# A local-attention layer with post-norm and a ternary FFN: scores on the whole array, o moved by DMA, FFN bias on ScalarE

## Chip, cores and metric

The kernel runs on one core of one Trainium2 chip. The metric is the device time of one execution in microseconds; the median of three runs is given for the kernel before.

## What is computed

For x of 16 sequences x 512 tokens x 256 features (all float32):

```python
qkv = (x @ Wqkv + bqkv).reshape(B, S, 3, H, Dh)          # 16 heads of 16
# blocks of 128 tokens; a query sees keys at most 128 positions away
scores = einsum('bhnqd,bhnkd->bhnqk', qb, kwin) * (1/16) # masked outside the band
out = einsum('bhnqk,bhnkd->bhnqd', softmax(scores), vwin)
x = layernorm(x + out @ Wout + bout)
h = relu(x @ quantise(W1).T + b1)                        # W1 (1024, 256), values -1, 0, 1
x = layernorm(x + h @ quantise(W2).T + b2)
```

## The kernel before

A **row** is one sequence of 512 tokens. The loop `steps` goes over rows; in the body of row b the attention of row b, the projections of row b+1 and the rest (output projection, norms, FFN) of row b-1 run side by side. One body has four **quads**, v = 0 to 3: quad v makes the scores of four heads of row b, and the row maxima of the four heads that come two quads later. Each quad has 12 **units** of scores (three for a head: blocks of 384, 384 and 2 x 256 columns) and 12 units of maxima; `weave` puts them at positions between the matmuls of the other steps, which the table `SIDE` lists for each quad. Before, positions come in runs of two units of both kinds.

Precision: matmul operands are split in a rounded part and a rest (`_hi`, `_lo`); ScalarE writes the first, VectorE the second, so nearly every PSUM result passes ScalarE and then VectorE before TensorE can use it.

The steps that matter here, with their engines:
- `scores` (L459) multiplies 50 of 128 partitions, `max_scores` (L475) 48 of them. The two lie in different halves of the partitions, since a quad and the one two quads later use different halves c. VectorE then adds the band to a unit of maxima and takes the row maximum (L812), ScalarE takes the exponential of a unit of scores (L670), GpSimd zeroes what is outside the band (`mask`, L973, L977).
- `pva`, `pvb` (L503): probabilities times v for the quad before, four column groups of 32 side by side. ScalarE copies the result to u (L714).
- `ut` (L513): four transposes of u, then VectorE takes the reciprocal of 16 sums per partition (L848) and multiplies (L852). `ot` (L543): eight transposes of the normalised o per row, then oT_hi on ScalarE, oT_lo on VectorE (L859), then the output projection `op` (L484).
- `ln1`, `x1`, `x1t` (L564): statistics on VectorE, rstd on GpSimd, x1 on both ScalarE and VectorE, eight transposes, x1T_hi and x1T_lo.
- `f1` (L578, L582): per 128 hidden units one matmul that adds the bias from a row of ones, then four of 256 columns; relu to hid_hi on ScalarE (L740), rest on VectorE (L895). `f2` (L595): 32 matmuls of 256 columns. `ln2` on VectorE and GpSimd (L1027).
- PSUM: two score banks, three for maxima, three shared by all other steps in turn. SyncE issues all DMAs in program order.

`dve_order` delays a VectorE piece by so many units of maxima as `LAG` says.

Of the kernel before, what the change touches and what calls it, by code (L numbers as in the profile page):

```python
# [21 lines left out]
F32 = mybir.dt.float32  # L22
F32R = mybir.dt.float32r
# [39 lines left out]
]  # L63

COST = {"qk": (3072, 6), "vp": (3072, 12), "op": (3072, 12), "ut": (1024, 4), "ot": (1024, 4), "x1t": (1024, 4),
        "nmt": (256, 1), "f1": (2560, 10), "f2": (8192, 32), "pva": (2200, 1), "pvb": (2200, 1)}
# [4 lines left out]
N_MAX = 3  # L71
RUN = 2
RUNS_AT = (0.5, 0.92)

LAG = {"ln1": 1, "ln2": 1, "qk": 1, "ot": 1, "x1t": 0, "f1": 0, "op": 1, "ut": 0, "f2": 1}
N_SHARED = 6 - N_MAX

USES_BANK = {"pva", "ut", "qk", "ot", "op", "vp", "x1t", "f1", "f2", "nmt"}
# [20 lines left out]
NEEDS = {"ot": "ut", "op": "ot", "f1": "x1t", "f2": "f1"}  # L99


def weave():

    out = []
    for v in range(QUADS):
        total = sum(COST.get(name_of(s), (0, 0))[0] for s in SIDE[v])
        units = []
        for i in range(UNITS):
            pos = (i // RUN * RUN + RUNS_AT[0]) / UNITS * total * RUNS_AT[1]
            units += [(pos, "scores", i), (pos, "max", i)]  # L110
# [11 lines left out]
WOVEN = weave()  # L122

# [9 lines left out]
def row_of(v, step, at):  # L133
# [9 lines left out]
    if name == "xr":  # L143
        return (0, None) if attn else None
# [17 lines left out]
def dve_order(v):  # L162
# [7 lines left out]
    for step, woven in zip(SIDE[v], WOVEN[v]):  # L170
# [9 lines left out]
        after = late[-1][0] + 1 if late and name_of(late[-1][1]) == name_of(step) in ("ln1", "ln2") else 0  # L180
# [12 lines left out]
def postln_layer(nc, xT, x, wqkv, bqk, bv, wout, bout, w1T, b1, w2T, b2, out):  # L193
    ctx = ExitStack()
    with ctx:
# [11 lines left out]
        B1 = sb("b1_rows", [P, FF], F32R)  # L207
        ONES2 = sb("ones_rows", [P, S // 2], F32R)
# [5 lines left out]
        ONES = sb("ones", [P, P])  # L214
# [5 lines left out]
        SK = sb("k_stack", [P, 8, S], F32R)  # L220
# [24 lines left out]
        ABS = sb("abs_sums", [P, 3])  # L245
        THR = sb("thresholds", [P, 4])
# [5 lines left out]
        PST = [bank("st_a"), bank("st_b")]  # L252
# [22 lines left out]
        s_small = sem("bqk_bv_in")  # L275
        s_const = sem("constants")
# [4 lines left out]
        s_b1 = sem("b1_lo_in")  # L281
# [800 lines left out]
```

## Time and profile before

| | |
|---|---|
| median of three runs | 1185.28 us (1185.11 to 1187.25) |
| profiled execution, its own time | 1187.86 us |
| its span | 1186.1 us |
| TensorE matmul busy | 1056.2 us, 89% |
| VectorE busy | 859.3 us, 72% |
| ScalarE busy | 613.3 us, 52% |
| GpSimd busy | 518.8 us, 44% |
| mean granted TensorE clock | 0.924 of full |

Busy time counts compute instructions alone. The clock has two levels, 1.2 GHz (0.5) and 2.4 GHz (1.0); a mean between them says how much of the time each was granted. A matmul's duration in the trace is its latency; how fast matmuls follow each other is read from their starts.

### The profile page before, as it was taken

The page shows a single profiled execution, that of the slowest core. Times are in us where ns is not written, and L with a number is a line of the kernel's source. Part 1 is how long each engine was busy: PE and PEld are TensorE (multiplying, and loading weights), DVE is VectorE, ACT ScalarE, POOL GpSimd, SP SyncE. Part 2 cuts the span into 40 slices and gives each one's busy share as a digit, 9 for nine tenths or more (in the row PEclk, how much of TensorE's full clock was granted, in tenths as well). Part 3 has the DMA queues.
Part 4 walks back from the last instruction along what each step waited for, and adds up shares of the span by engine and source line. Part 5 has one row for each costly group of instructions (what it writes and reads, how often), then busy time and mean ns, then how long its engine had stood idle before and what let it go on. Part 6 is the DMA issues. An engine that isn't in the chain of part 4 may idle for free.

```text
span 1186.1 us, 23520 instructions
## 1 busy us (share of the span) xinstructions
PE 1056.2 (89%) x8132; PEld 771.9 (65%) x8132; DVE 859.3 (72%) x2934; ACT 613.3 (52%) x1258; POOL 518.8 (44%) x824
## 2 busy tenths in 40 slices
PE   4778899999989899998989999898989999897966
PEld 3444676766767576676767666676767667675755
DVE  3975777778787777778777777877777787777333
ACT  4154554655455564556455555545655554555421
POOL 2124353544535445463535445453535445344430
PEclk9677899998989999898999989898998989898889
DMA  5835255434354443444344534424554342442000
GB/s 169 108 54 92 28 82 82 68 70 73 58 75 68 83 73 76 61 80 65 56 82 73 88 61 78 75 37 82 82 82 68 69 74 57 57 69 56 1 19 18
DMA packets 56999, 81.49 MB, mean 69 GB/s; under 512 B 7729, under 2 KB 27697, under 8 KB 56882
## 3 DMA queue, kind: packets, MB, share of 16 engines
q1 hardware_dynamic: 56882, 80.00, 40.3%
q8 instruction: 66, 1.08, 0.4%
q14 instruction: 51, 0.42, 0.2%
HBM read 20.19 MB, written 8.39 MB: 24 GB/s over the span
## 4 chain that ended last, share of the span: by engine, by line
PE 77%; DVE 13%; issue 4%; POOL 2%; ACT 2%; DMA 1%; SPq 0%; POOLq 0%; DVEq 0%; ACTq 0%
PE shared L484 18%; PE st_a L459 13%; PE shared L503 12%; PE shared L595 11%; PE shared L582 10%; DVE mx L812 5%; PE st_b L459 5%; PE shared L578 3%; PE shared L564 3%; DVE oT_lo L859 2%; POOL ln_rstd L1007 1%; PE shared L543 1%; PE mx L475 1%; DVE qk_lo L839 1%; DVE rmax L812 1%
## 5 line engine op out<-in xcount | busy, mean ns | idle before, releaser
L812 DVE CUSTOM_DVE_ANT_0 mx<-mx,band 128x384 f32<-128x384 f32 (+1 forms) x1024 | 480.1, 514 | 187.0 <-PE mx L475 182.6
L670 ACT ACTIVATE probs<-st_a 128x384 f32<-128x384 f32 (+1 forms) x384 | 202.0, 526 | 371.3 <-PE st_a L459 367.7
L475 PE MATMUL mx<-k_stack,q_stack 48*128 48x384 f32 (+1 forms) x1024 | 273.0, 369 | 8.0 <-DMA k_stack<-qk_lo 3.9
L973 POOL TENSOR_SCALAR_AFFINE_SELECT probs<-probs 128x512 f32<-128x512 f32 (+1 forms) x256 | 128.8, 527 | 317.5 <-ACT probs L670 316.3
L670 ACT ACTIVATE probs<-st_b 128x384 f32<-128x384 f32 (+1 forms) x384 | 200.8, 523 | 0.0
L459 PE MATMUL st_a<-q_stack,k_stack 50*128 50x384 f32 (+1 forms) x512 | 186.9, 406 | 3.1 <-ACT probs L670 2.4
L475 PEld LDWEIGHTS mx<-k_stack,q_stack 48*128 48x128 f32 x1024 | 165.7, 201 | 13.2 <-DVE rmax L812 8.7
L503 PE MATMUL shared<-probs,v_aug 128*32 128x384 f32 (+1 forms) x2048 | 161.2, 445 | 0.7 <-DVE x L902 0.7
L459 PEld LDWEIGHTS st_a<-q_stack,k_stack 50*128 50x128 f32 x512 | 90.3, 197 | 104.2 <-issue 63.5
L812 DVE DVE_READ_ACCUMULATOR2_ANT rmax<- 128x1 f32 x1024 | 144.5, 141 | 0.0
L459 PE MATMUL st_b<-q_stack,k_stack 50*128 50x384 f32 (+1 forms) x512 | 143.2, 320 | 0.0
L582 PE MATMUL shared<-x1T_hi,w1q 128*128 128x256 f32 x512 | 142.9, 295 | 0.0
L582 PE MATMUL shared<-x1T_lo,w1q 128*128 128x256 f32 x512 | 138.5, 288 | 0.0
L595 PE MATMUL shared<-w2q,hid_hi 128*128 128x256 f32 x512 | 131.9, 293 | 4.1 <-DVE hid_lo L895 4.1
L595 PE MATMUL shared<-w2q,hid_lo 128*128 128x256 f32 x512 | 131.8, 293 | 0.0
L977 POOL TENSOR_SCALAR_AFFINE_SELECT probs<-probs 128x512 f32<-128x512 f32 (+1 forms) x256 | 127.1, 520 | 0.0
L895 DVE SCALAR_TENSOR_TENSOR hid_lo<-shared,hid_hi 128x512 fp32r<-128x512 f32 x128 | 87.9, 687 | 36.0 <-ACT hid_hi L740 34.6
L740 ACT ACTIVATE hid_hi<-shared 128x512 fp32r<-128x512 f32 x128 | 76.8, 600 | 59.4 <-PE shared L582 59.4
L595 PEld LDWEIGHTS shared<-w2q,hid_hi 128*128 128x128 f32 x512 | 97.7, 191 | 14.7 <-issue 10.2
L582 PEld LDWEIGHTS shared<-x1T_hi,w1q 128*128 128x128 f32 x512 | 99.4, 194 | 10.5 <-issue 7.7
L503 PEld LDWEIGHTS shared<-probs,v_aug 128*32 128x32 f32 x2048 | 57.7, 111 | 68.2 <-issue 50.7
L595 PEld LDWEIGHTS shared<-w2q,hid_lo 128*128 128x128 f32 x512 | 97.4, 190 | 6.9 <-issue 2.9
(107 smaller groups left out, 1965.3 us busy)
## 6 DMA issues: line engine op xcount, KB each, us to landing
q_stack<-qk_hi SPq DMA_DIRECT2D x128, 128.0 KB, 4.3
k_stack<-qk_hi SPq DMA_DIRECT2D x128, 128.0 KB, 5.2
x_raw<-in_xT SPq DMA_DIRECT2D x16, 512.0 KB, 5.7
q_stack<-qk_lo SPq DMA_DIRECT2D x64, 128.0 KB, 3.9
k_stack<-qk_lo SPq DMA_DIRECT2D x64, 128.0 KB, 5.5
y<-in_x SPq DMA_DIRECT2D x16, 512.0 KB, 6.1
out<-x SPq DMA_DIRECT2D x32, 256.0 KB, 2.1
probs<-in_w2T SPq DMA_DIRECT2D x1, 1024.0 KB, 10.6
```

What stands on the lines that cost most here:

```text
L459: mm = pe.matmul(PST[i % 2][:, col:col + n], SK[rows, hd, W * m:W * m + W], SQ[rows, hd, q0:q0 + n], start=True, stop=True)
L475: mm = pe.matmul(PMX[i % N_MAX][:, col:col + n], SQ[rows, hd, W * m:W * m + W], SK[rows, hd, k0:k0 + n], start=True, stop=True)
L484: mm = pe.matmul(ps, lhs(a, kc), rhs(z, kc), start=(n == 0), stop=(n == len(terms) - 1))
L503: mm = pe.matmul(G[32 * g:32 * g + 32, q0:q0 + width], VAUG[:, vq, m, g, :], PR[:, vq % 2, g // 2, lo:lo + width], start=(m == 0), stop=(m ...
L582: mm = pe.matmul(ps, W1Q[:, kc, P * f:P * f + P], X1T[a][:, kc, 256 * hf:256 * hf + 256], start=False, stop=(kc == KC - 1 and a == 1))
L595: mm = pe.matmul(G[:, D * t:D * t + D], HID[a][:, f, P * t:P * t + P], W2Q[:, f, :], start=(f == 0 and a == 0), stop=(f == FC - 1 and a == 1))
L670: act.activation(PR[:, v % 2, g // 2, lo:lo + n], PST[i % 2][:, 0:n], ACT.Exp, scale=SCALE) \
L740: act.activation(HID[0][:, 2 * p:2 * p + 2, :].rearrange("p f t -> p (f t)"), G[:, :], ACT.Relu).then_inc(s_hh, 1)
L812: mx = dve.tensor_tensor_reduce(ps, ps, band, 1.0, -3e38, ALU.add, ALU.max, RMAX[:, g, m:m + 1])
L895: dve.scalar_tensor_tensor(pair[1], G[:, :], 0.0, pair[0].bitcast(F32), ALU.max, ALU.subtract).then_inc(s_hl, 1)
L973: pool.affine_select(out=pr_before, in_=pr_before, compare_op=ALU.is_ge, fill=0.0, base=0, pattern=[[0, n], [1, W]], channel_multiplier=-1)
L977: last = pool.affine_select(out=pr_after, in_=pr_after, compare_op=ALU.is_ge, fill=0.0, base=0, pattern=[[0, n], [-1, W]], channel_multipl ...
```

## The change

- `scores` and `max_scores` use all partitions: k gets one stack for each half, zero in the other half (`SK[0]`, `SK[1]`), so 128 rows (scores) or 112 (maxima) are multiplied. The scores of a quad now also wait for the stacks of the other half.
- Three score banks, three for maxima, two shared. Units stand one by one: `SCORES_AT`, `MAXIMA_AT` in place of runs.
- `ut` and `ot` on TensorE are gone. v lies in the even columns of `VAUG` and ones in the odd ones, so u has o in even partitions and the sums in odd ones; two DMAs per quad (`columns`) bring them to `OC` and `SC`. A new step `od` (twice per row) takes the reciprocal of 128 x 512 sums on VectorE and multiplies: on VectorE for half 1, on GpSimd for half 0. oT_hi and oT_lo read `OC`.
- `f1` has no bias matmul: ScalarE makes relu with bias in two halves (to U or H32), then copies it to hid_hi; VectorE subtracts from SBUF. The shared bank is free after the relu.
- The neg_max transpose goes to a bank of the maxima. ln1's rstd is made in two halves.
- `SIDE` and `LAG` are new.

```diff
 SIDE = [
-    [("qk", 0), "nmt", "pva", "pvb", ("vp", 0), "ut", ("vp", 1), ("ot", 0), ("ot", 1), ("qk", 1), ("op", 0),
-     ("op", 1)],
...
+    [("qk", 0), "nmt", ("ot", 0), "pva", "pvb", ("qk", 1), ("od", 1)],
+    [("ot", 1), ("qk", 2), ("op", 0), ("ln1", 0), ("op", 1), ("ln1", 1), "nmt", ("ln1", 2), ("ln1", 3), ("vp", 0),
+     ("x1", 0), ("x1", 1), "pva", "pvb", ("x1", 2), ("x1", 3), ("qk", 3), ("vp", 1), ("x1t", 0), ("xs", 0),
+     ("x1t", 1)],
+    ["nmt", ("f1", 0, 0), ("f1", 0, 1), ("f1", 0, 2), "pva", "pvb", ("f1", 0, 3), ("xs", 1), ("f2", 0),
+     ("ln2", 0)],
+    [("ln2", 1), ("f1", 1, 0), "xr", ("od", 0), ("f1", 1, 1), ("f1", 1, 2), ("f1", 1, 3), ("f2", 1), ("ln2", 2),
+     "nmt", ("ln2", 3), "pva", "pvb"],
 ]
-LAG = {"ln1": 1, "ln2": 1, "qk": 1, "ot": 1, "x1t": 0, "f1": 0, "op": 1, "ut": 0, "f2": 1}
+LAG = {"ln1": 1, "ln2": 0, "qk": 1, "od": 3, "ot": 1, "x1t": 1, "f1": 0, "op": 2, "f2": 0}
...
+            def columns(r, vq):
+                i, q = vq // 2, 4 * r + vq
+                rows = slice(64 * (vq % 2), 64 * (vq % 2) + 64)
+                sp.wait_ge(s_u, q + 1)
...
+                sp.dma_start(OC[rows, i, :], U[0:P:2, :]).then_inc(s_uin, 16)
+                sp.dma_start(SC[rows, :], U[1:P:2, :]).then_inc(s_uin, 16)
...
-                    mm = pe.matmul(PST[i % 2][:, col:col + n], SK[rows, hd, W * m:W * m + W],
-                                   SQ[rows, hd, q0:q0 + n], start=True, stop=True)
+                    mm = pe.matmul(PST[i % N_SCORE][:, col:col + n], SK[c][:, hd, W * m:W * m + W],
+                                   SQ[:, hd, q0:q0 + n], start=True, stop=True)
...
-                        pe.matmul(ps, B1[:, P * f:P * f + P], ONES2[:, :], start=True, stop=False)
...
+                    for k, f in enumerate((2 * p, 2 * p + 1)):
+                        last = act.activation(H[:, 256 * k:256 * k + 256], G[:, 256 * k:256 * k + 256], ACT.Relu,
+                                              bias=B1C[:, f:f + 1])
+                    last.then_inc(s_hr, 1)
+                    act.wait_ge(s_hr, n + 1)
+                    act.activation(HID[0][:, 2 * p:2 * p + 2, :].rearrange("p f t -> p (f t)"), H[:, :],
+                                   ACT.Identity).then_inc(s_hh, 1)
...
+                elif name == "od":
+                    i = step[1]
+                    dve.wait_ge(s_uin, 128 * r + 64 * i + 64)
+                    dve.reciprocal(SC[:, :], SC[:, :]).then_inc(s_rc, 1)
+                    if i == 1:
+                        dve.wait_ge(s_rc, 2 * r + 2)
+                        dve.tensor_tensor(OC[:, i, :], OC[:, i, :], SC[:, :], ALU.mult).then_inc(s_od, 1)
...
-                    dve.scalar_tensor_tensor(pair[1], G[:, :], 0.0, pair[0].bitcast(F32), ALU.max,
-                                             ALU.subtract).then_inc(s_hl, 1)
+                    dve.tensor_tensor(pair[1], (U, H32)[p % 2][:, :], pair[0].bitcast(F32), ALU.subtract) \
+                        .then_inc(s_hld, 1)
...
+                elif step == ("od", 0):
+                    pool.wait_ge(s_rc, 2 * r + 1)
+                    pool.tensor_tensor(OC[:, 0, :], OC[:, 0, :], SC[:, :], ALU.mult).then_inc(s_od, 1)
```

**Place 1: VectorE, from the end of quad 0 into quad 1, where o is finished** (ISA with mx is a unit of row maxima, rmax its read-out). Before:

```order
L848 RECIPROCAL recip<-shared 128x16 [waits o_norm_done,uT_full]
L852 TENSOR_TENSOR o_norm<-shared,recip 128x4x64 [waits recip_done]
L812 ISA mx,rmax<-mx,band 128x384 [waits max_scores_full]
L812 ISA rmax 128x1
L812 ISA mx,rmax<-mx,band 128x384 [waits max_scores_full]
L812 ISA rmax 128x1
L812 ISA mx,rmax<-mx,band 128x256 [waits max_scores_full]
L812 ISA rmax 128x1
L812 ISA mx,rmax<-mx,band 128x256
L812 ISA rmax 128x1
L859 SCALAR_TENSOR_TENSOR oT_lo<-shared,bv_cols,oT_hi 128x512 [waits oT_hi_done] x2
```

Of the change:

```order
L916 SCALAR_TENSOR_TENSOR qk_lo<-shared,bqk,qk_hi 128x512 [waits qk_hi_done]
L922 RECIPROCAL sums_cols<-sums_cols 128x512 [waits u_and_sums_in]
L925 TENSOR_TENSOR o_cols<-o_cols,sums_cols 128x512 [waits recip_done]
L889 ISA mx,rmax<-mx,band 128x384 [waits max_scores_full,neg_max_done]
L889 ISA rmax 128x1
L929 SCALAR_TENSOR_TENSOR oT_x1T_lo<-o_cols,bv_cols,oT_x1T_hi 128x512 [waits oT_hi_done]
```

Before, a reciprocal of 16 elements stands alone and three units of maxima lie between it and the rests of o. Now one of 512 elements and the multiplication follow the rest of qk1, and the second rest of o comes one unit later.

**Place 2: VectorE, at the start of quad 3, among the rests of the hidden layer.** Before:

```order
L852 TENSOR_TENSOR o_norm<-shared,recip 128x4x64 [waits recip_done]
L895 SCALAR_TENSOR_TENSOR hid_lo<-shared,hid_hi 128x512 [waits hidden_hi_done]
L812 ISA mx,rmax<-mx,band 128x384 [waits max_scores_full,neg_max_done]
L812 ISA rmax 128x1
L812 ISA mx,rmax<-mx,band 128x384 [waits max_scores_full]
L812 ISA rmax 128x1
L895 SCALAR_TENSOR_TENSOR hid_lo<-shared,hid_hi 128x512 [waits hidden_hi_done]
```

Of the change:

```order
L966 TENSOR_TENSOR hid_lo<-u,hid_hi 128x512 [waits hidden_hi_done]
L889 ISA mx,rmax<-mx,band 128x384 [waits max_scores_full]
L889 ISA rmax 128x1
L922 RECIPROCAL sums_cols<-sums_cols 128x512 [waits u_and_sums_in]
L889 ISA mx,rmax<-mx,band 128x256 [waits max_scores_full]
L889 ISA rmax 128x1
L889 ISA mx,rmax<-mx,band 128x256
L889 ISA rmax 128x1
L966 TENSOR_TENSOR hid_lo<-hidden,hid_hi 128x512 [waits hidden_hi_done]
L889 ISA mx,rmax<-mx,band 128x384 [waits max_scores_full]
L889 ISA rmax 128x1
L966 TENSOR_TENSOR hid_lo<-u,hid_hi 128x512 [waits hidden_hi_done]
```

The other reciprocal of 512 elements now stands between the first rest and the other three of this half.

**Place 3: TensorE, from the transposes of x1 to the FFN** (quad 1 into quad 2). Before:

```order
L564 MATMUL shared<-identity,x 128x128
L484 MATMUL shared<-xT_hi,wqkv_hi 128x512 [waits o_norm_done]
L484 MATMUL shared<-xT_hi,wqkv_lo 128x512
L484 MATMUL shared<-xT_lo,wqkv_hi 128x512
L484 MATMUL shared<-xT_hi,wqkv_hi 128x512
L459 MATMUL st_a<-q_stack,k_stack 128x384 [waits exp_done]
L475 MATMUL mx<-k_stack,q_stack 128x384 [waits max_read]
```

Of the change:

```order
L529 MATMUL st<-q_stack,k_stack_top 128x256 [waits exp_done,v_next_done]
L529 MATMUL st<-q_stack,k_stack_top 128x256
L629 MATMUL shared<-identity,x 128x128 x4
L588 MATMUL mx<-identity,neg_max 72x128 [waits neg_max_done]
L643 MATMUL shared<-oT_x1T_hi,w1q 128x256 [waits x1T_lo_done,x1T_hi_done]
L643 MATMUL shared<-oT_x1T_lo,w1q 128x256
L643 MATMUL shared<-oT_x1T_hi,w1q 128x256 [waits x1T_lo_done,x1T_hi_done]
```

Before, the whole projection qk3 and two runs of units lie between the last transpose and the first FFN matmul (L578 follows two more matmuls later). Now only the small transpose of neg_max does.

## Rows read from the trace of the kernel before

**Rows 1.** chain of waits, starts of one row and the next (start us, us, what)

```profile
454.31 0.50 PE shared L484
...
522.50 0.50 PE shared L484
```

**Rows 2.** busy time by stage, one whole row (us, then each engine's busy us, clock, DMA share)

```profile
454.31:522.50 68.19, 63.43 (x508) 46.57 (x509) 52.53 (x183) 37.69 (x78) 32.42 (x51) 0.95 0.44 72
```

**Rows 3.** waits of TensorE in that row, largest first, and the last of five

```profile
PE shared L564 <- ACT x L727: 1.5, 1, 1.5
PE shared L513 <- ACT u L714: 1.4, 1, 1.4
...
PE shared L484 <- DVE qk_lo L839: 0.2, 1, 0.2
```

**Rows 4.** busy time by stage around the transposes of x1 (granted clock third from the right)

```profile
481.20:482.60 1.40, 0.00 (x0) 0.01 (x1) 1.40 (x7) 1.22 (x3) 1.40 (x4) 0.51 0.00 0
...
485.33:488.05 2.72, 2.72 (x11) 1.88 (x11) 1.90 (x7) 1.25 (x3) 2.16 (x1) 0.50 0.01 3
488.05:491.00 2.95, 2.95 (x25) 2.41 (x21) 2.71 (x10) 2.21 (x4) 1.99 (x5) 1.00 0.34 92
```

**Rows 5.** timeline of TensorE, one run of units between FFN matmuls (start us, us)

```profile
500.37 0.28 PE L595 MATMUL shared<-w2q,hid_lo 128*128 128x256 f32 x1
500.49 0.28 PE L595 MATMUL shared<-w2q,hid_hi 128*128 128x256 f32 x1
500.70 0.38 PE L459 MATMUL st_a<-q_stack,k_stack 50*128 50x256 f32 x1
500.71 0.38 PE L475 MATMUL mx<-k_stack,q_stack 48*128 48x256 f32 x1
...
501.04 0.33 PE L459 MATMUL st_b<-q_stack,k_stack 50*128 50x384 f32 x1
...
501.32 0.39 PE L595 MATMUL shared<-w2q,hid_lo 128*128 128x256 f32 x1
501.54 0.28 PE L595 MATMUL shared<-w2q,hid_hi 128*128 128x256 f32 x1
```

**Rows 6.** timeline of TensorE, 512 columns and probabilities times v

```profile
524.29 0.39 PE L484 MATMUL shared<-xT_hi,wqkv_lo 128*128 128x512 f32 x1
524.52 0.39 PE L484 MATMUL shared<-xT_lo,wqkv_hi 128*128 128x512 f32 x1
...
524.95 1.28 PE L503 MATMUL shared<-probs,v_aug 128*32 128x256 f32 x16
526.17 0.38 PE L459 MATMUL st_a<-q_stack,k_stack 50*128 50x256 f32 x1
```

**Rows 7.** chain of waits, the transposes of u and of o

```profile
530.75 0.44 PE shared L513 x4
...
533.35 0.87 PE shared L543 x8
```

**Rows 8.** groups by line and shape (busy us, mean ns | idle before), VectorE, ScalarE, TensorE

```profile
L812 DVE DVE_READ_ACCUMULATOR2_ANT rmax<- 128x1 f32 x1024 | 144.5, 141 | 0.0
...
L895 DVE SCALAR_TENSOR_TENSOR hid_lo<-shared,hid_hi 128x512 fp32r<-128x512 f32 x128 | 87.9, 687 | 36.0 <-ACT hid_hi L740 34.6
...
L578 PE MATMUL shared<-ones_rows,b_rows 128*128 128x256 f32 x256 | 80.8, 315 | 3.8 <-DVE x1T_lo L889 2.0 <-DVE hid_lo L895 0.4
L740 ACT ACTIVATE hid_hi<-shared 128x512 fp32r<-128x512 f32 x128 | 76.8, 600 | 59.4 <-PE shared L582 59.4
...
L852 DVE TENSOR_TENSOR o_norm<-shared,recip 128x256 f32<-128x256 f32 x64 | 27.2, 425 | 2.2
...
L848 DVE RECIPROCAL recip<-shared 128x16 f32<-128x16 f32 x64 | 15.9, 249 | 6.4 <-PE shared L513 6.4
```

**Rows 9.** groups by line and shape, GpSimd: mask and second norm

```profile
L973 POOL TENSOR_SCALAR_AFFINE_SELECT probs<-probs 128x512 f32<-128x512 f32 x128 | 82.9, 647 | 317.5 <-ACT probs L670 316.3
...
L1027 POOL TENSOR_SCALAR x<-x,ln_mv,ln_rstd 128x256 f32<-128x256 f32 x60 | 73.1, 1224 | 3.2
```

More of the change, by code:

```diff
@@ L106, in weave @@
         total = sum(COST.get(name_of(s), (0, 0))[0] for s in SIDE[v])
[L107 to L110, printed above, removed]
+        units = [((i + SCORES_AT[0]) / UNITS * total * SCORES_AT[1], "scores", i) for i in range(UNITS)]
+        units += [((i + MAXIMA_AT[0]) / UNITS * total * MAXIMA_AT[1], "max", i) for i in range(UNITS)]
+        units.sort()
         at, slot = 0, []
@@ L122, with units_before, ffn_steps_in_u @@
 WOVEN = weave()
+def units_before(v, step, kind):
+    return sum(k == kind for woven in WOVEN[v][:SIDE[v].index(step)] for _, k, _ in woven)
+NMT_AT = [units_before(v, "nmt", "max") for v in range(QUADS)]
+assert max(NMT_AT) < UNITS
+def ffn_steps_in_u():
+    out, n, last = [], 0, 0
+    for v in range(QUADS):
+        for step in SIDE[v]:
+            if name_of(step) == "f1":
+                n += 1
+                last = n if step[2] % 2 == 0 else last
+            if step == "pvb":
+                out.append(last)
+    return out
+U_FFN = ffn_steps_in_u()
 def stages(at):
@@ L179, in dve_order @@
                 due(maxima)
-        after = late[-1][0] + 1 if late and name_of(late[-1][1]) == name_of(step) in ("ln1", "ln2") else 0
+        after = late[-1][0] + 1 if late and name_of(late[-1][1]) == name_of(step) == "ln2" else 0
         late.append((max(maxima + LAG.get(name_of(step), 0), after), step))
@@ L449, in scores @@
                 c, hd = v // 2, 4 * (v % 2) + g
-                rows = slice(64 * c, 64 * c + 50)
                 if i == 0:
@@ L466, in max_scores @@
                 c, hd = v // 2, 4 * (v % 2) + g
-                rows = slice(64 * c, 64 * c + 48)
+                rows = slice(0, 112)
                 if i == 0:
@@ L471, in max_scores @@
                     pe.wait_ge(s_mxr, 12 * (4 * r + v) + i - N_MAX + 1)
+                if i == NMT_AT[(v + 2) % 4] and not (first and v == 0):
+                    pe.wait_ge(s_nmt, 4 * r + v)
                 for m in BLOCKS[u]:
@@ L751, in step @@
                             other_weights()
+                        row = row_of(v, step, at)
+                        before = name_of(step) in ("f1", "nmt", "pvb", "x1t")
+                        if row is not None and before:
+                            side_work(v, step, b, *row, at)
                         for _, kind, i in woven:
@@ L754, in step @@
                                 exp(b, v, i, at)
-                        row = row_of(v, step, at)
-                        if row is not None:
+                        if row is not None and not before:
                             side_work(v, step, b, *row, at)
@@ L890, in side_work @@
                         .then_inc(s_x1l, 1)
-                elif name == "f1":
+                elif name == "f1" and step[2] not in REST_ON_POOL:
                     hf, p = step[1], step[2]
```

310 lines of the change are left out of this document (167 added, 143 removed), and 6 rows, old and new, of the table SIDE.

## The prediction

> **What bounds the kernel now.** I read the page first: TensorE is busy 89% of the span, VectorE 72%. The chain of waits gives the period: the same matmul of qk0 starts at 454.31 and at 522.50 us [rows 1], so a row of the batch costs 68.2 us, and 15.5 such rows (the first has no FFN yet, the last no projections) stand between a start and an end of some 50 us each. Within one row TensorE is busy 63.4 us, VectorE 52.5, ScalarE 37.7, at a mean clock of 0.95 [rows 2]. The waits of TensorE inside it are five and sum to 4.7 us; the largest are for x1 and for u [rows 3]. The clock is lost in one place: around the wait for x1 it falls to the 1.2 GHz level, and from 482.6 to 488.05 TensorE works at half rate [rows 4], 5.4 us that would take 2.7. So 68.2 = 60.8 of matmuls at full clock + 4.7 of waits + 2.7 of clock. TensorE bounds the kernel, through its own work and through short chains over ScalarE, VectorE and GpSimd.
>
> **Full-array scores: no gain by themselves.** A score matmul and a maxima matmul start together, at 500.70 and 500.71 us, since they lie in different halves of the array [rows 5]. That is lost. What is won is the passage between half and full array: from the last FFN matmul before the run (500.49) to the second after it (501.54) are 1.05 us, less two FFN spacings of 0.12 leaves 0.81 for 896 columns of each kind, which alone stream in 0.37. Matmuls on the whole array follow each other in 0.12 us for 256 columns [rows 5] and 0.23 for 512 [rows 6], so I take 0.175 for 384. A head then costs 2 x (2 x 0.175 + 2 x 0.12) = 1.18 us and 16 heads 18.9. Before, 24 runs of about 0.79 are 18.9. I cost it at nothing. The waits for the other half's stacks also cost nothing: the maxima of that quad need the same stack at the same time.
>
> **What TensorE is rid of, per row.** 16 bias matmuls of 0.12: 1.9 us. 16 transposes of u at 0.44 for four: 1.8. Eight of o: 0.9 [rows 7, 8]. Against it, each `pva` and `pvb` (1.22 us for 16 matmuls [rows 6]) now stands between full-array matmuls, where half of these borders were shared with a run of units before: 0.2 us at each of eight, less what was there, 1.4. Net 3.2. The waits of rows 3 and the fallen clock go with their chains: after the change both halves of vp, qk3 and the two pv halves lie behind the output projection (3 x 1.4 + 2.8 us, and units), against a chain of some 5 us. That frees 3.2 + 4.7 + 2.7 = 10.6 us and leaves 57.6.
>
> **What comes in.** The costly piece is the reciprocal of 128 x 512 on VectorE, twice per row. The trace has only one of 128 x 16, 249 ns [rows 8]. VectorE takes 425 ns for 256 elements and 687 for 512, so 1.02 ns per element and 163 fixed; a reciprocal of 16 at that pace would take 179. It takes 70 more. If that excess is per element, it is 5.4 ns each and 512 take 2.9 us; with the fixed part of the shortest VectorE row, 141 ns, it is 6.8 ns and 3.6 us. Bounds: 0.69 us (one pass, the excess a constant) and 8.0 us (249 x 32). I take R = 3.3, between the two readings that fit the row. The Trainium skill, "VectorE: DVE Perf Modes", section "Walkthrough: the 8-slice pipeline in each mode", says that reciprocal is an iterated divide with a repeat count of 8; at eight passes R would be 4.3 and the sum below 2.0 us per row longer. The row shows an excess, but not its slope.
>
> Where R bites, per row:
> - Place 1, end of quad 0. Behind the last matmul of qk1 come 0.5 us of hand-overs, qk1_hi and qk1_lo (0.6 + 0.69, as hid_hi and hid_lo [rows 8]), R, the product 0.69, oT_hi 0.6 and oT_lo 0.69, and only then the second half of the output projection. That is 3.8 + R. TensorE has qk2, three units and three matmuls of `op` meanwhile, 2.2 us. Wait: 1.6 + R = 4.9. The two DMAs of u land earlier: `pvb` ends 5.5 us before `op`.
> - Place 2, start of quad 3. Three rests of the hidden layer and the units of maxima queue behind R; TensorE waits for a bank of maxima, then for each rest. With R of one pass the wait is 0.7 (ScalarE now needs about 1.25 us per FFN step for two relus of about 0.38, an estimate between half and whole of its 0.6 for 512 columns [rows 8], overlapped, and a copy of 0.6, besides the exponentials); it grows by what R exceeds that. Wait: about R, 3.3.
> - Place 3. After the second four transposes nothing covers x1T_hi, the copy of x that stands between the two on ScalarE, and x1T_lo: 1.9 us.
> - The last mask of quad 3 now queues on GpSimd behind two norms of 1.22 us and takes two large and two small selects, 2 us [rows 9]: `pva` of quad 0 waits 0.5. The end of f1 in quad 2: 0.3.
> - The clock: one fall as now, since a wait of 4.9 us is longer than the two of 1.4 and 1.5 around which it falls today: 2.7.
>
> VectorE's own load is then 52.5 - 2.6 (four small reciprocals and products) + 2 x 3.3 + 0.7 = 57.2 us, just under TensorE's 57.6, so it has little slack to catch up with. ScalarE goes to about 44. Start and end of the program: qk1 comes earlier, so the first stack does (4 us won), and the last o has DMA and R on its way (4 lost). Nothing.
>
> **Sum.** 57.6 + 4.3 + 2R + 2.7 = 71.2 us for R = 3.3, 3.0 more than now; times 15.5 is 46.5. The profiled execution took 1187.9, so 1234.4; the median of the three runs lies 2.6 lower: **1232 us**. The change decides at R = 1.8 us, or at 3.1 if the clock stays up.
>
> **Rivals.**
> - *The reciprocal costs about one pass* (0.7). For it: the excess on 16 elements may be pipeline depth. Then 57.6 + 4.3 + 1.4 = 63.3 and the clock stays up, since no wait is over 2.3 us: 76 us less, 1109. Chance 0.13.
> - *R is long but covered.* TensorE and VectorE each have 57 us of work, and the banks let TensorE run three units ahead; if half of the waits of places 1 and 2 fall together with others, and the clock falls less, a row takes about 65: 1136. For it: the waits are added here one after another, and a wait at one place lets the others catch up. Against: at place 1 the order leaves TensorE 2.2 us of work whatever went before. Chance 0.21.
> - *The clock does not fall.* 68.5 per row, 1190. Chance 0.08, half of it near no change.
> - *R is longer, or the clock falls twice* (places 1 and 2). R = 4.4 gives 73.4 per row, 1266; two falls 73.9, 1274. For it: a fixed part of 112 ns, below every VectorE row here, is what it takes. Chance 0.20. The count of eight in the Trainium skill, on the page named above, would lead here.
> - *The full array does not do what I say.* If 384 columns alternate slower than 0.175, it adds at most 0.05 x 64 = 3 us per row, inside the range.
>
> **Numbers.** The forecast itself has 0.38, and 1200 to 1262 as its own range. The range leaves out half of the cheap reciprocal and the worst of the last but one case: 1115 to 1282. A measurement tells 0.2% (2.4 us). Faster: 0.13 + 0.21 + 0.02 = 0.36; same 0.04; slower 0.60.
>
> **What would show it.** After: RECIPROCAL x32 near 3.3 us mean; a wait of TensorE for oT_lo near 5 us in each row; waits for hid_lo and rmax in quad 3; a wait for x1T_lo of 1 to 2; period near 71; a clock below 1.0 behind `op`. Wrong if the reciprocal takes under 1.8 us, if its waits are found but sum to under 4 us per row, or if matmuls on the whole array alternate at another spacing.

## Result and profile after

The changed kernel takes 1306.93 us (median of 4 runs, 1302.94 to 1310.77), the kernel before 1186.26 us beside it (1185.11 to 1187.25). The ratio is 1.1017, 95% interval 1.0971 to 1.1064: slower by 10.2%. The forecast was 1232 with a range to 1282: the right side, 75 us too low.

The profiled execution took 1303.41 us, its span is 1301.6. First the page: busy time by engine, the granted clock in 40 slices, and the chain that ended last by engine and by line.

```profile
PE 1072.4 (82%) x7492; PEld 872.0 (67%) x7492; DVE 958.1 (74%) x2853; ACT 723.7 (56%) x1513; POOL 567.0 (44%) x904
...
PEclk9787997989898898989878898898979989898978
...
PE 57%; DVE 19%; DMA 10%; ACT 7%; issue 3%; SPq 2%; POOL 1%; POOLq 0%; DVEq 0%; ACTq 0%
```

TensorE does less work than before (no bias matmuls, no transposes of u and o), yet shows more busy time, 1072.4 against 1056.2 us (a matmul at the lower clock is busy for longer). DMA holds 10% of the chain. The chain of waits over one row of the batch shows where (start us, us, what):

```profile
471.13 3.21 DVE sums_cols L922
...
475.10 0.73 DVE hid_lo L966
...
476.36 1.17 DVE hid_lo L966
...
495.00 0.61 ACT u L777
...
496.20 6.80 DMA sums_cols<-u
503.02 3.36 DVE sums_cols L922
506.41 0.70 DVE o_cols L925
507.14 0.73 ACT oT_x1T_hi L786
507.89 0.76 DVE oT_x1T_lo L929
508.79 1.41 PE shared L558 x5
...
546.74 3.21 DVE sums_cols L922
```

Both reciprocals stand in the chain, as forecast, but at place 1 a transfer of 6.80 us stands in front of one. The row is 546.74 - 471.13 = 75.6 us long (68.2 in [rows 1]). Over eight rows, by the issues of x on SyncE, the mean is (874.11 - 259.79) / 8 = 76.8 us:

```profile
259.79 0.74 SPq L434 DMA_DIRECT2D x_raw<-in_xT  x1
...
874.11 0.51 SPq L434 DMA_DIRECT2D x_raw<-in_xT  x1
```

Busy time by stage, for this row and for 300 to 900 us (length, then busy us of PE, PEld, DVE, ACT, POOL, then granted clock, DMA share, GB/s; it answers to [rows 2]):

```profile
471.13:546.74 75.61, 65.28 (x470) 53.73 (x469) 58.60 (x178) 44.68 (x95) 35.24 (x57) 0.93 0.45 78
300.00:900.00 600.00, 513.45 (x3644) 423.17 (x3644) 458.10 (x1378) 348.43 (x734) 275.32 (x433) 0.90 0.46 78
```

The same stretch of the kernel before:

```profile
300.00:900.00 600.00, 557.47 (x4452) 409.01 (x4450) 462.74 (x1608) 330.50 (x684) 286.83 (x453) 0.95 0.43 71
```

With 76.8 and 68.2 us for a row, TensorE is without a matmul for 11.1 us of a row (4.8 before) and busy for 65.7 (63.4 before), at a clock of 0.90 (0.95). The waits of TensorE over the whole span (us in total, times, longest; [rows 3] shows one row of before):

```profile
PE shared L558 <- DVE oT_x1T_lo L929: 70.1, 16, 9.3
PE mx L547 <- DMA k_stack_bottom<-qk_lo: 39.2, 15, 3.9
PE mx L547 <- DVE rmax L889: 29.4, 20, 3.4
PE shared L657 <- DVE hid_lo L966: 15.2, 29, 2.4
PE shared L643 <- DVE oT_x1T_lo L960: 13.3, 29, 0.7
```

Places 1, 2 and 3 are there: 70.1, then 29.4 + 15.2, then 13.3. The second row is a wait that the forecast did not have. The totals hold the start of the program too (the 9.3 is there). From 300 to 900 us, 7.8 rows, the same list reads:

```profile
PE shared L558 <- DVE oT_x1T_lo L929: 30.4, 8, 4.9
PE mx L547 <- DMA k_stack_bottom<-qk_lo: 22.2, 8, 3.7
PE mx L547 <- DVE rmax L889: 12.4, 8, 1.6
PE shared L643 <- DVE oT_x1T_lo L960: 6.5, 14, 0.7
PE shared L577 <- issue: 5.3, 8, 0.7
PE shared L657 <- DVE hid_lo L966: 4.9, 11, 0.8
```

The row with "issue" names no releaser. It stands in front of `pva` of quad 0, and in the row above GpSimd's last select for quad 3 ended at 491.13 and `pva` began at 491.23, so it is read here as the wait for the last mask. The groups by line and shape that answer to [rows 8]:

```profile
L922 DVE RECIPROCAL sums_cols<-sums_cols 128x512 f32<-128x512 f32 x32 | 107.2, 3350 | 57.6 <-DMA sums_cols<-u 57.6
...
L966 DVE TENSOR_TENSOR hid_lo<-u,hid_hi 128x512 fp32r<-128x512 f32 x64 | 68.0, 1062 | 38.7 <-ACT hid_hi L816 38.7
...
L812 ACT ACTIVATE u<-shared,b_cols 128x256 f32<-128x256 f32 x128 | 53.6, 472 | 47.3 <-PE shared L643 46.8 <-DVE hid_lo L966 0.5
```

The reciprocal takes 3350 ns. VectorE idles 57.6 us in front of 15 of them, until the sums arrive (2.4 us in the row above). What the DMA engines do then is in the issues of SyncE (start us, us) and in the windows of that time (next to last number: mean share of the 16 engines, 1.00 is all of them):

```profile
489.24 0.49 SPq L486 DMA_DIRECT2D out<-x  x1
489.78 0.50 SPq L434 DMA_DIRECT2D x_raw<-in_xT  x1
490.43 0.61 SPq L427 DMA_DIRECT2D q_stack<-qk_hi  x1
...
493.65 0.73 SPq L427 DMA_DIRECT2D k_stack_bottom<-qk_lo  x1
...
496.20 0.59 SPq L482 DMA_DIRECT2D sums_cols<-u  x1
```

```profile
490.00:496.00 6.00, 5.33 (x50) 3.29 (x49) 4.41 (x17) 4.36 (x10) 3.83 (x10) 1.00 1.04 219
496.00:503.00 7.00, 4.54 (x23) 3.73 (x22) 4.15 (x17) 3.10 (x7) 2.69 (x7) 0.92 0.77 112
```

Within 7 us SyncE issues a store, the 512 KB of x and the six transfers of a stack, and then those of u. The engines are full from 490 to 496, and the sums need 6.8 us from issue to landing, where the median of all 64 such transfers is 2.9. The Trainium skill, "DMA: Bandwidth & Descriptors", section "Issuing engines are not separate DMA queues", says that all DMAs end on the same 16 engines whoever issues them; the trace agrees as far as it goes, since all of these come from one queue and share those engines.

The clock falls three times in this row, not once (the granted clock is the third number from the right; 0.5 is 1.2 GHz): at 478 behind the waits of place 2, at 502 behind the wait for the third stack (2.5 us), and at 509 behind that for the second rest of o (3.2 us). In the 2 us ahead of 502 TensorE was busy for 0.17 us, in those from 506 to 508 not at all. In windows of 0.5 us from 256 to 870 us, eight rows, there are 20 such falls; eight rows of the kernel before have 8.

```profile
478.00:480.00 2.00, 2.00 (x10) 1.85 (x9) 1.90 (x8) 0.83 (x3) 1.23 (x3) 0.51 0.00 0
...
500.00:502.00 2.00, 0.17 (x1) 0.17 (x2) 0.66 (x1) 0.00 (x0) 1.31 (x4) 0.99 0.29 57
502.00:504.00 2.00, 2.00 (x6) 1.71 (x7) 0.98 (x1) 0.00 (x0) 0.00 (x0) 0.50 0.87 181
...
506.00:508.00 2.00, 0.00 (x0) 0.00 (x0) 1.71 (x5) 0.86 (x2) 0.00 (x0) 1.00 0.82 93
...
510.00:512.00 2.00, 2.00 (x11) 2.00 (x11) 0.93 (x5) 0.27 (x1) 0.00 (x0) 0.50 0.00 0
```

### The profile page after: what moved, and what is told of

Its sections match the earlier page's. It is cut to its first block, busy times and chain, and to the rows that moved or that the text cites. A ratio compares the mean times of both kernels' runs of the same rounds, so it can differ in the third digit from the quotient of the medians.

```text
span 1301.6 us, 23064 instructions
## 1 busy us (share of the span) xinstructions
PE 1072.4 (82%) x7492; PEld 872.0 (67%) x7492; DVE 958.1 (74%) x2853; ACT 723.7 (56%) x1513; POOL 567.0 (44%) x904
## 4 chain that ended last, share of the span: by engine, by line
PE 57%; DVE 19%; DMA 10%; ACT 7%; issue 3%; SPq 2%; POOL 1%; POOLq 0%; DVEq 0%; ACTq 0%
PE shared L558 12%; PE shared L577 11%; PE st L529 9%; PE mx L547 9%; DMA sums_cols<-u 8%; PE shared L657 8%; DVE sums_cols L922 8%; PE shared L643 6%; DVE hid_lo L966 4%; DVE mx L889 3%; ACT hid_hi L816 2%; SPq L427 1%; ACT hidden L812 1%; ACT u L812 1%; DVE oT_x1T_lo L929 1%
## 5 line engine op out<-in xcount | busy, mean ns | idle before, releaser
L731 ACT ACTIVATE probs<-st 128x384 f32<-128x384 f32 (+1 forms) x768 | 382.9, 523 | 240.9 <-PE st L529 238.8
L547 PE MATMUL mx<-k_stack_bottom,q_stack 112*128 112x384 f32 (+1 forms) x512 | 156.0, 347 | 42.6 <-DMA k_stack_bottom<-qk_lo 39.2
L547 PE MATMUL mx<-k_stack_top,q_stack 112*128 112x384 f32 (+1 forms) x512 | 153.2, 346 | 33.3 <-DVE rmax L889 27.2
L657 PE MATMUL shared<-w2q,hid_hi 128*128 128x256 f32 x512 | 149.1, 310 | 18.3 <-DVE hid_lo L966 15.2
L643 PE MATMUL shared<-oT_x1T_hi,w1q 128*128 128x256 f32 x512 | 141.8, 292 | 15.7 <-DVE oT_x1T_lo L960 13.3
L529 PE MATMUL st<-q_stack,k_stack_top 128*128 128x384 f32 (+1 forms) x512 | 151.0, 337 | 4.0 <-ACT v_next L762 3.5
L547 PEld LDWEIGHTS mx<-k_stack_bottom,q_stack 112*128 112x128 f32 x512 | 101.0, 207 | 77.1 <-DMA k_stack_bottom<-qk_lo 46.1
L529 PE MATMUL st<-q_stack,k_stack_bottom 128*128 128x384 f32 (+1 forms) x512 | 148.7, 332 | 3.4 <-ACT u L812 3.4
L922 DVE RECIPROCAL sums_cols<-sums_cols 128x512 f32<-128x512 f32 x32 | 107.2, 3350 | 57.6 <-DMA sums_cols<-u 57.6
L643 PE MATMUL shared<-oT_x1T_lo,w1q 128*128 128x256 f32 x512 | 137.7, 283 | 0.0
L657 PEld LDWEIGHTS shared<-w2q,hid_hi 128*128 128x128 f32 x512 | 106.7, 208 | 27.8 <-issue 13.3
L529 PEld LDWEIGHTS st<-q_stack,k_stack_top 128*128 128x128 f32 x512 | 98.9, 206 | 24.6 <-issue 12.9
```

Of the source, the lines that this page charges most:

```text
L529: mm = pe.matmul(PST[i % N_SCORE][:, col:col + n], SK[c][:, hd, W * m:W * m + W], SQ[:, hd, q0:q0 + n], start=True, stop=True)
L547: mm = pe.matmul(PMX[i % N_MAX][:, col:col + n], SQ[rows, hd, W * m:W * m + W], SK[c][rows, hd, k0:k0 + n], start=True, stop=True)
L643: mm = pe.matmul(G[:, 256 * k:256 * k + 256], W1Q[:, kc, P * f:P * f + P], X1T[a][:, kc, 256 * hf:256 * hf + 256], start=(kc == 0 and a == ...
L657: mm = pe.matmul(G[:, D * t:D * t + D], HID[a][:, f, P * t:P * t + P], W2Q[:, f, :], start=(f == 0 and a == 0), stop=(f == FC - 1 and a == 1))
L731: act.activation(PR[:, v % 2, g // 2, lo:lo + n], PST[i % N_SCORE][:, 0:n], ACT.Exp, scale=SCALE) \
L922: dve.reciprocal(SC[:, :], SC[:, :]).then_inc(s_rc, 1)
```

## Experiments

Each is named by its label. "Before" is 1186 to 1191 us in all of them. e1, e2, e3, f1 and h4 leave the inversion of the sums out (of both halves or of one), f3 leaves the bias b1 out; all others compute everything. Medians, and ratios to before with 95% interval:

| run | us | ratio to before |
|---|---|---|
| changed kernel | 1306.9 | 1.102 (1.097 to 1.106) |
| e1 both reciprocals light | 1224.5 | 1.022 (1.013 to 1.030) |
| e2 half 1 light | 1238.8 | 1.043 (1.039 to 1.047) |
| e3 half 0 light | 1288.1 | 1.082 (1.077 to 1.087) |
| e4 load of x later | 1263.4 | 1.064 (1.059 to 1.069) |
| f1 = e4 + e1 | 1181.3 | 0.996 (0.994 to 0.997) |
| f2 = e4, half-array scores in runs | 1304.8 | 1.100 (1.097 to 1.103) |
| f3 before, no bias matmuls | 1140.7 | 0.962 (0.960 to 0.963) |
| f4 = e4, projection later | 1288.4 | 1.085 (1.082 to 1.089) |
| g1 before, two more reciprocals | 1315.5 | 1.108 (1.105 to 1.112) |
| g2 = e4, half 0 in pieces | 1265.7 | 1.067 (1.065 to 1.069) |
| g3 = e4, half 1 by tokens | 1241.0 | 1.044 (1.039 to 1.048) |
| g4 = g2 + g3 | 1245.9 | 1.051 (1.048 to 1.054) |
| h1 = e4, pv between f1 and f2 | 1312.7 | 1.104 (1.100 to 1.109) |
| h2 = h1, half 1 by tokens, 2nd part behind qk2 | 1283.8 | 1.079 (1.075 to 1.083) |
| h3 = h2, half 0 in pieces | 1266.0 | 1.065 (1.060 to 1.069) |
| h4 = h1, both light | 1225.0 | 1.030 (1.026 to 1.035) |
| i1 = h3, store later | 1190.0 | 1.002 (0.999 to 1.005) |
| i2 = g3, store later | 1259.5 | 1.061 (1.056 to 1.066) |

### The reciprocal, and the transfer in front of it

```diff
-                    dve.reciprocal(SC[:, :], SC[:, :]).then_inc(s_rc, 1)
+                    dve.tensor_scalar(SC[:, :], SC[:, :], 0.01, None, ALU.mult).then_inc(s_rc, 1)
```

> Both reciprocals of 128x512 are replaced by one multiplication by a constant, so the sums are not inverted; everything else, the DMAs too, is as in the changed kernel. Theory A (the reciprocal's length is the loss, added up as forecast): R falls from 3.35 to about 0.5, so 2 x 2.8 us per row go, 5.7 x 15.5 = 88 us, and another 42 us if the clock then stays up: 1219, or 1177. Theory B (beside it the transfers of u are late behind x and the stacks, 8 us instead of 3): the same 88 us go but the wait for the transfer stays, so TensorE still waits for the rest of o some 3 us per row, the clock still falls, and the time is near 1220. Theory C (other waits take the place): less than 50 us go, over 1255.

> Only the reciprocal of half 1 (place 1, end of quad 0) is replaced by a multiplication by a constant. Theory A: its wait is in series with TensorE, so 2.8 x 15.5 = 44 us go, 1263; more if the clock no longer falls behind the output projection. Theory C (the chain catches up elsewhere): under 20 us.

> Only the reciprocal of half 0 (place 2, quad 3, ahead of the rests of the hidden layer) is replaced by a multiplication by a constant. Theory A: the wait there was about R, so some 2.6 x 15.5 = 40 us go, 1267, and the waits for hid_lo and rmax behind it vanish. Theory C (place 2 is mostly covered, TensorE has units ahead there): under 20 us, over 1287.

The light operation takes 435 ns. Half 1 is worth 68 us, more than its own length (2.9 us x 15.5 = 45) and more than was expected (44), half 0 only 19, less than the 40 of theory A there, both together 82. Place 1 is in series with TensorE. Place 2 is not a matter of the reciprocal alone, as the waits of TensorE in e3 show:

```profile
PE shared L657 <- DVE hid_lo L969: 35.0, 34, 1.9
...
```

The wait for the row maxima (29.4 us) is gone but for 4.9, and that for the rests of the hidden layer has grown from 15.2 to 35.0. How such a rest gets late is in the timeline of e1 (start us, us, engine, line):

```profile
510.34 0.63 ACT L816 ACTIVATE hid_hi<-u 128x512 fp32r<-128x512 f32 x1
510.48 2.39 POOL L1072 TENSOR_TENSOR y<-y,bout_rep 128x1024 f32<-128x1024 f32 x1
...
511.01 2.42 DVE L966 TENSOR_TENSOR hid_lo<-u,hid_hi 128x512 fp32r<-128x512 f32 x1
```

The rest of the hidden layer now has both inputs in SBUF (before, one was in PSUM, 687 ns [rows 8]). Undisturbed it takes 0.69 us; this one began at 511.01 behind a GpSimd instruction that ran to 512.87, and ended at 513.43, 0.56 after it. The Trainium skill, "SBUF — State Buffer", section "SBUF: two separate sides", says that a VectorE instruction with two SBUF inputs and a GpSimd one that reads SBUF exclude each other for the whole instruction; the row agrees. The rests that read U take 1062 ns in the mean in the changed kernel and 1324 in e1, the others 749 and 855.

> The load of x (512 KB), issued on SyncE ahead of the third stack at the start of quad 0, is issued behind the two DMAs of u of that quad instead; the reciprocals are whole. Theory B (transfers of u and of the stack are late because the DMA engines are full with x and the stack): sums land some 2 to 3 us earlier and the maxima wait less for the stack, 2.5 x 15 = 38 us less, 1269, or half of that. Theory A alone (the reciprocal is all): no change, 1300 to 1310. A third possibility is that x is then late for its own split in quads 1 and 2: slower.

```diff
+                    if v == 0 and nxt2 and at >= 0:
+                        load_x()
```

(behind `columns` of quad 0 instead of at the head of the body.) 43 us less, and the waits in question shrink from 57.6 and 39.2 us to these:

```profile
DVE sums_cols L927 <- DMA sums_cols<-u: 14.4, 10, 10.5
...
PE mx L552 <- DMA k_stack_bottom<-qk_lo: 2.5, 6, 1.1
```

So the late transfers were a cause of their own, worth 43.5/15.5 = 2.8 us per row. The gain came through the third stack and the clock, not through the wait for the rest of o: that one rose from 70.1 to 83.0 us, probably since TensorE no longer stood still ahead of it. By the issues of x a row is 73.5 us, 3.2 less, of which waits are 1.8 and the clock 1.7 (it now falls 16 times in eight rows).

> The load of x behind the DMAs of u, and both reciprocals replaced by a multiplication by a constant (the sums are not inverted). Additive theory: x later gave 43 us and the light operations 82, so 1307 - 125 = 1182. Overlap theory (both sit in one chain, u to rest of o, and what remains is covered once one is gone): more than 1195. The forecast's floor (57.6 of matmuls per row, 4.3 of waits, R 0.5) would give 1100 to 1120; if the time is near 1180 instead, 4 to 5 us per row of that floor are missing and must be found among the waits or the matmuls.

1181.3: additive to a microsecond (1306.9 - 43.5 - 82.4 = 1181.0). Both causes hold, and do not hide each other. What is left of the change, with x later and reciprocals that cost nearly nothing, is worth 0.4%.

```diff
+                    if vq % 2 == 1:
+                        dve.reciprocal(DUM[:, :], DUM[:, :]).then_inc(s_dum, 1)
```

> The kernel before with one more reciprocal of 128x512 on VectorE at the head of the normalisation of u, twice per row (for the last quad of each half), on a tile that nothing else reads. It takes 3.35 us. Theory A (a reciprocal of this length in the chain from u to o costs its own length, whatever the kernel): 2 x 3.35 x 15.5 = 104 us more, 1290. Theory C (the order before has slack behind the transposes of u that hides a part; only the changed order bares it): 30 to 70 us more. Under 30: the reciprocal's length matters only together with the DMA.

The other way round, 128 us more on the kernel before, above the 104 of the plain sum. The two agree less than they seem to. By the issues of x a row is 75.9 us, 7.7 more; from 300 to 900 us the waits of TensorE grew by 3.4 of them, only half of the 6.7 that were put in, and the clock took 3.7 (the mean of the span is 0.885, 0.924 before). How much of the other half is slack of the order and how much is TensorE working slower beside the chain is not told apart.

### The parts on TensorE

```diff
-                    mm = pe.matmul(PST[i % N_SCORE][:, col:col + n], SK[c][:, hd, W * m:W * m + W],
-                                   SQ[:, hd, q0:q0 + n], start=True, stop=True)
+                    mm = pe.matmul(PST[i % N_SCORE][:, col:col + n], SK[c][srows, hd, W * m:W * m + W],
+                                   SQ[srows, hd, q0:q0 + n], start=True, stop=True)
...
+            pos = (i // 2 * 2 + 0.5) / UNITS * total * 0.92
+            units += [(pos, "scores", i), (pos, "max", i)]
```

> The changed kernel with the load of x later, its scores put back on half of the array (partitions 64 c to 64 c + 64, maxima 48 rows) in runs of two units of both kinds as before; all else as in e4_x_later (1263). Theory F (as forecast, the whole array is worth nothing in matmul time): 1255 to 1275. Theory G (the whole array costs time, since scores and maxima no longer share it): over 20 us less, under 1243. Theory H (single units on the whole array gain, by smoother work for VectorE and ScalarE or fewer passages): over 1285.

The form of the change (whole array and single units together) is worth 41 us in this order (theory H). Busy time by stage, f2 and then e4:

```profile
300.00:900.00 600.00, 507.49 (x3692) 361.48 (x3685) 464.98 (x1398) 341.57 (x739) 279.83 (x444) 0.93 0.43 77
```

```profile
300.00:900.00 600.00, 524.13 (x3810) 432.46 (x3809) 479.83 (x1442) 365.49 (x770) 291.01 (x458) 0.93 0.47 81
```

By the issues of x a row is 75.9 us in f2 and 73.5 in e4, so TensorE is busy for 507.49/600 x 75.9 = 64.2 and 524.13/600 x 73.5 = 64.2 us of a row: the same. The gain lies in the waits, 11.7 against 9.3 us. The whole array shows no saving of matmul time. Whether the array or the single units instead of runs of two save the waits, this one run does not tell apart, since its edit changed both.

```diff
-                        pe.matmul(ps, B1[:, P * f:P * f + P], ONES2[:, :], start=True, stop=False)
```

> The kernel before without its bias matmuls in the first FFN matmul (b1 is left out of the result, nothing takes its place). Theory F (TensorE bounds, each of 16 matmuls per row is worth 0.12): 1.9 x 16 = 30 us less, 1157. Theory W (the time is set by chains at the FFN's ends): less than 12 us.

45 us, not 30. A row is 65.0 us by the issues of x, 3.2 less, but most of that is clock (0.99 from 300 to 900 us against 0.95): 2.9 us per row were lost to it before and 0.5 are now. The waits are 0.3 less, and the matmuls at full clock only 0.6 (60.5 to 59.9, by the sum of "Why the prediction was wrong"), not 1.9. So the edit was worth more than its work because it ended most falls of the clock.

### Orders

```diff
-    [..., ("qk", 1), ("od", 1)],
-    [("ot", 1), ("qk", 2), ("op", 0), ...
+    [..., ("qk", 1)],
+    [("qk", 2), ("od", 1), ("vp", 0), ("ot", 1), ("op", 0), ...
```

> The changed kernel with the load of x later and another order at the end of quad 0: the reciprocal and product of half 1 stand behind qk2, and half of vp stands ahead of the rests of o and the output projection (instead of behind it). Theory A (place 1 is a wait of u's transfer plus R with 2.2 us of work beside it): 1.4 us of vp and its units, some 2 us, lie beside the chain more, so 2 x 15.5 = 31 us less than e4_x_later, 1232, and more if the clock stays up. Theory S (ScalarE's and VectorE's queues, blocked at that wait, stop the exponentials and the maxima, and that is the wait): up to 50 us less. If the work taken from behind the projection bares the norm chain there: no gain.

25 us slower than e4 where 31 less were expected. The wait for the rest of o grew from 83.0 to 92.4 us although work was put in front of it. The reciprocal itself now stands behind qk2, which is the likely reason.

```diff
+                        if pieces and kind == "max":
+                            piece()
...
+                c = slice(128 * k, 128 * k + 128)
+                rec = dve.reciprocal(SC[:, c], SC[:, c])
```

> The changed kernel with the load of x later (1263), and the reciprocal of half 0 in quad 3 done in four pieces of 128 columns, one ahead of each of the next four units of maxima, instead of in one piece. The work is the same plus three fixed parts. If place 2 is a matter of blocking (rests of the hidden layer and maxima behind one long instruction), the gain is most of what the light operation gave there (19 us): 1246 to 1255. If it is a matter of VectorE's work: no gain, 1263 or slightly more.

Nothing, with the same exchange as e3: the wait for the maxima fell from 29.4 to 5.9 us, that for hid_lo rose from 13.4 to 40.4. Pieces of 128 elements take 944 ns, 256 take 1750 (g3).

```diff
+                c = slice(256 * k, 256 * k + 256)
+                dve.reciprocal(SC[:, c], SC[:, c]).then_inc(s_rcp, 1)
+                dve.wait_ge(s_rcp, 2 * r + k + 1)
+                dve.tensor_tensor(OC[:, 1, c], OC[:, 1, c], SC[:, c], ALU.mult).then_inc((s_odp, s_od)[k], 1)
```

> The changed kernel with the load of x later, and reciprocal, product, rounded part and rest of half 1 done for tokens 0 to 255 first, then for the others; the first half of the output projection needs only the first. The chain from u to the first matmul that needs it gets shorter: R/2 and half of the three others, less one fixed part each, 2.4 us. Theory A (place 1 is that chain in series with TensorE): 2.4 x 15.5 = 37 us less, 1226, and up to 20 more if the clock falls less. If VectorE's total load decides: 1263 or more.

22 us instead of 37: the wait for o fell from 83.0 to 46.4, but one of 20.1 for the rest of qk2 came in its place, which stood behind the second part.

> Both of the two edits above on the changed kernel with x later. If they are independent, as x and the light reciprocals were: their gains add, some 1210. If a common bound (VectorE with 58 us of work in a row of 68) takes over: above 1225.

1245.9 against 1241.0 of g3, whose runs spread from 1234.6 to 1257.6: no gain beside it, and no sure loss. Not independent.

```diff
-    ["nmt", ("f1", 0, 0), ("f1", 0, 1), ("f1", 0, 2), "pva", "pvb", ("f1", 0, 3), ("xs", 1), ("f2", 0),
+    ["nmt", ("f1", 0, 0), ("f1", 0, 1), ("f1", 0, 2), ("f1", 0, 3), "pva", "pvb", ("xs", 1), ("f2", 0),
...
-    [..., ("f1", 1, 3), ("f2", 1), ("ln2", 2), "nmt", ("ln2", 3), "pva", "pvb"],
+    [..., ("f1", 1, 3), "nmt", "pva", "pvb", ("f2", 1), ("ln2", 2), ("ln2", 3)],
```

> The changed kernel with the load of x later, and in quads 2 and 3 pva and pvb (2.4 us and their units) moved between the last matmuls of f1 and the first of f2, as the kernel before has them. If the chain relu, relu, copy, rest behind the last f1 is a bound of its own, its cover gives up to 1 us per row in quad 2 and little in quad 3, where the reciprocal is still in front: 1245 to 1258. If place 2 is the reciprocal alone: 1263.

> h1_pv_between with half 1 by tokens, the second part behind the copy and the rest of qk2 instead of ahead of them. If the wait for the rest of qk2 in g3_tokens (20 us, a bank that was freed late) was given to this order, the edit now gives some 37 us instead of 22: 1210 to 1220.

> h2_tokens_deferred with the reciprocal of half 0 in four pieces. With the cover of pva and pvb behind f1 the pieces should now give what they did not alone, 10 to 19 us: 1195 to 1210. If the pieces again give nothing, place 2 is bound by VectorE's own work.

> h1_pv_between with both reciprocals replaced by a multiplication by a constant (the sums are not inverted). Against f1_x_later_both_light (1181) it shows what the chain at the end of f1 costs when no reciprocal stands in front: its waits for hid_lo were 35 us, so 20 to 35 us less, 1146 to 1161. It would mean that the rest of the change is worth 25 to 40 us against the kernel before, and the two reciprocals take that and more. If it stays at 1181, the rest of the change is worth nothing.

All four are 55 to 64 us above the top of what the move was expected to give. The waits for hid_lo fell to under 3 us, as meant, but those for the maxima rose (29.4 to 55.1 us in h1), and TensorE now waited 61 us for the third stack. The steps between them were nearer: 29 us by tokens (37 expected), and 18 for the pieces (10 to 19 expected), which alone had given nothing. Against f1 (1181.3), h4 is 44 us slower with that wait in it, so it does not answer what it was made for. The issues of SyncE in h1:

```profile
490.17 0.39 SPq L491 DMA_DIRECT2D out<-x  x1
490.71 0.60 SPq L427 DMA_DIRECT2D q_stack<-qk_hi  x1
...
493.93 0.61 SPq L427 DMA_DIRECT2D k_stack_bottom<-qk_lo  x1
```

The store of the second half of the output stands in SyncE's program order ahead of the stack. It waits for the second norm, which waits for f2, and f2 had been moved behind pva and pvb.

```diff
-                if post:
+                if at == B:
                     store(b, 1)
...
+                    if v == 0 and at > 1:
+                        store(b - 1, 1)
```

(behind `columns` of the next quad 0.)

> h3_all (1266) with the store of the second half of the output issued on SyncE behind the two DMAs of u in the next quad 0, instead of ahead of the third stack. If the store is what makes the stack late, the wait of 61 us for k_stack_bottom goes and the time with it, to 1200 to 1215. If the stack waits for its own conditions, no change.

> g3_tokens (1241) with the same move of the store. There the wait for that stack is only 3 us in all, so the move itself should give little; but the stack's six transfers then start up to 2 us earlier and are out of the way of u's: 0 to 20 us less, 1221 to 1241.

i1 is 1190.0, 76 us less than h3: the store was the cause, and more than its 61 us came back, since the clock rose too (0.948 over the span against 0.932). It computes all that the changed kernel does, and stands level with the kernel before (0.999 to 1.005); no version that computes everything beat the kernel before. In the order of g3 the same move cost 18 us, where 0 to 20 less were expected. There the wait of VectorE for the sums changed little (15.6 to 10.7 us), that of TensorE for the rest of qk2 rose from 20.1 to 33.6, and the clock from 300 to 900 us fell from 0.95 to 0.93. Why an earlier stack should do that stays open.

## Why the prediction was wrong

The profiled execution took 69 us more than the 1234.4 that the sum gave for it. The terms, per row:

| | forecast | measured |
|---|---|---|
| waits | 10.9 (4.3 + 2R) | 11.1 |
| clock | 2.7 | 5.9 |
| matmuls at full clock | 57.6 | 59.8 |
| row | 71.2 | 76.8 |

The clock's 5.9 is the sum of busy time x (1 - granted clock) over windows of 1 us from 300 to 900 us, 45.8 us, divided by 7.8 rows; the kernel before gives 2.9 by the same sum. 5.6 us x 15.5 rows are 87; start and end together are 18 shorter than before, where the forecast said nothing (1301.6 - 15.5 x 76.8 = 111 against 1186.1 - 15.5 x 68.2 = 129).

- **R was right.** 3.35 us against 3.3. It decides the sign, as said: without it (e1) 82 of the 120 us go, and two of them on the kernel before (g1) make such a loss. The repeat count of 8 in the Trainium skill ("VectorE: DVE Perf Modes", section "Walkthrough: the 8-slice pipeline in each mode"), read as eight passes, would have given 4.3, an estimate; the row of 3350 ns decides.
- **The step that failed first is "The two DMAs of u land earlier"**, and with it "The waits for the other half's stacks also cost nothing". In the row shown the sums land 6.8 us after their issue, at 503.02, with VectorE idle for the last 2.4, because a stack and x are in front of them; and the stack itself is late and holds TensorE for 2.8 us per row (22.2/7.8) ahead of place 1. "The maxima of that quad need the same stack at the same time" was no reason to cost it at nothing. The trace of before has x and a stack close together too, but there nothing in quad 0 waited for a transfer. I took the time of a transfer as that of a lonely one. e4 puts 43 us on it.
- **"The clock: one fall as now: 2.7" is the largest miss of the sum**, 3.2 us per row or 50 us: 5.9, by 20 falls in eight rows. Places 1 and 2 each make one, the wait for the stack a third. Two falls were a rival (73.9 us, 1274), with the right cause; the third was in no rival. With x later the stack's fall is gone, place 1 is 39.1/8.2 = 4.8 us per row (forecast 4.9), and the row is 73.5 us and the time 1263: near that rival, though with fewer waits and more of matmuls than it had. The rival of the cheap reciprocal let the clock stay up "since no wait is over 2.3 us"; [rows 3] and [rows 4] already showed a fall around waits of 1.4 and 1.5.
- **The waits agree in sum by luck.** From 300 to 900 us place 1 is 30.4/7.8 = 3.9 us per row (forecast 4.9), place 2 17.3/7.8 = 2.2 (3.3), place 3 0.8 (1.9), the last mask 0.7 (0.5); the third stack, 2.8, was not in the sum.
- **"What TensorE is rid of"** failed too, by 2.2 us per row or 34 us: of 3.2 us some 0.7 shows (59.8 against 63.4 - 2.9 = 60.5 before). f3 shows the same in the kernel before, 0.6 of the 1.9 of the bias matmuls, and f1, without the long reciprocals, has 60.2 where the forecast has 57.6. What takes it back is not resolved; the longer tails of matmuls in front of waits are counted as busy, which is a guess.
- **Start and end** together were 129 us before, not the "some 50 us each" of the forecast, and 111 after. That hid 18 us of the miss.
- **Full-array scores at nothing** fits TensorE's busy time (64.2 and 64.2) and missed what the new form does for the waits (f2, 41 us in this order). It is not what the forecast missed, since the old form would have been slower still.
- **hid_lo** was taken to keep its 687 ns. The half of them that reads U has a mean of 1062, and the row of e1 shows one held by a GpSimd instruction. That this is the second bound at place 2, and why half 0 alone gave 19 us and its pieces nothing, is argued and not shown: no run took the GpSimd work away. What h2 and h3 show is that with other work behind the last f1 the pieces do give 18 us.

## What to carry to other kernels

Where a change puts a DMA into a chain that was on engines alone, take its length from a transfer that shares the queue's neighbours: list what SyncE issues in the 10 us ahead of it, and move what is not urgent (here a load, later a store) behind it. A long instruction in a serial chain costs waits and then the clock; count both, and cover it by splitting the data that the next matmul needs first. And before an order is changed, follow each in-order queue past the moved step: a store that waits for a late norm held up six transfers that had nothing to do with it.

## What the runs showed of the hardware

- VectorE's reciprocal is linear in the elements per partition: 249 ns for 16 [rows 8], 944 for 128, 1750 for 256, 3350 for 512. That is some 150 ns and 6.25 ns for each element of a partition, about six times the 1.02 ns of a one-pass operation.
- A subtraction with two SBUF inputs took 0.69 us alone and up to 2.42 us with a GpSimd instruction under way, ending some 0.6 us behind it.
- Two reciprocals of 3.35 us per row cost the kernel before 128 us and not 104, of 7.7 us per row 3.7 by the clock; 16 bias matmuls of 0.12 less gave 45 and not 30, of 3.2 us per row 2.3 by the clock. In this kernel, with its short waits, the granted clock made about half of the one cost and most of the other gain.
